# LoRA A to the head of SyncE's queue, six folds before the first tile, and the fifth tile prepared between the second and third chunk of the second expert

## The reference

```python
y   = einsum('bsi,boi->bso', x, weight[adapter_ids])      # 16 experts of 1024 x 1024
h   = einsum('bsd,nrd->nbsr', y, lora_A)                  # 8 adapters of rank 16
out = x + (y @ W.T + bias) + einsum('nbsr,nor->bso', h, lora_B * (SCALE * lora_weights))
```

## Time and profile before

| | us |
|---|---|
| median of 3 runs | 1508.62 (1508.57 to 1510.61) |
| the profiled execution, its own time | 1511.33 |
| the profiled execution, span of its instructions | 1509.7 |
| TensorE busy with matmuls | 1492.8 (99%) |
| VectorE busy | 788.1 (52%) |
| ScalarE busy | 393.2 (26%) |
| GpSimd busy | 464.4 (31%) |

### The profile page before, as it was taken

One profiled execution on the slowest core, in us unless ns is written; L12 is line 12 of the kernel. 1 busy time (PEld: TensorE's weight loads), 2 busy tenths in 40 slices (PEclk: granted clock), 3 DMA queues, 4 the chain that ended last, 5 costly groups with the idle time before them and its releaser, 6 DMA issues.

```text
span 1509.7 us, 29738 instructions
## 1 busy us (share of the span) xinstructions
PE 1492.8 (99%) x6354; PEld 1190.2 (79%) x6355; DVE 788.1 (52%) x1192; ACT 393.2 (26%) x493; POOL 464.4 (31%) x651
## 2 busy tenths in 40 slices
PE   7999999999999999999999999999999999999998
PEld 4878888888888888878788888888888888888887
DVE  7767766367777368378842333333333333333331
ACT  5244343234444244244430111111111111111110
POOL 4365433533344433534102121221211212212111
PEclk9999999999999999999999999999999999999999
DMA  9979866667787467469744555555555555555553
GB/s 279 293 202 246 221 170 164 186 185 201 202 228 197 142 185 189 156 202 239 192 148 130 142 143 140 136 148 140 133 145 141 138 143 139 144 141 134 146 139 84
DMA packets 172705, 257.90 MB, mean 171 GB/s; under 512 B 31616, under 2 KB 135552, under 8 KB 172672
## 3 DMA queue, kind: packets, MB, share of 16 engines
q1 hardware_dynamic: 128896, 138.62, 36.5%
q10 hardware_dynamic: 23360, 73.28, 16.4%
q0 software_dynamic: 20416, 45.65, 10.9%
HBM read 181.93 MB, written 75.50 MB: 171 GB/s over the span
## 4 chain that ended last, share of the span: by engine, by line
PE 94%; DVE 3%; DMA 1%; ACT 1%; issue 1%; SPq 0%; DVEq 0%; POOL 0%; ACTq 0%; POOLq 0%
PE ps L751 31%; PE ps L755 31%; PE ps L758 31%; DVE w_turn L529 1%; DMA a_sb<-in_L_ffn_lora_A_dram 1%; DMA weff<-fold_sb 1%; DVE w_lo L586 1%; DVE fold_sb L644 1%; DVE x_turn L617 0%; ACT x_hi L409 0%; ACT w_hi L401 0%; PE ps L731 0%; DVE x_lo L624 0%; ACT fold_sb L441 0%; SPq L215 0%
## 5 line engine op out<-in xcount | busy, mean ns | idle before, releaser
L751 PE MATMUL ps<-w_hi,x_hi 128*128 (+1 forms) x2096 | 533.4, 395 | 2.9 <-issue 2.9
L755 PE MATMUL ps<-w_hi,x_lo 128*128 (+1 forms) x2096 | 531.4, 394 | 0.0
L758 PE MATMUL ps<-w_lo,x_hi 128*128 (+1 forms) x2096 | 531.2, 394 | 0.0
L751 PEld LDWEIGHTS ps<-w_hi,x_hi 128*128 128x128 f32 x2096 | 392.8, 188 | 101.8 <-issue 5.4
L755 PEld LDWEIGHTS ps<-w_hi,x_lo 128*128 128x128 f32 x2096 | 392.5, 187 | 97.0
L758 PEld LDWEIGHTS ps<-w_lo,x_hi 128*128 128x128 f32 x2096 | 392.2, 187 | 96.8
L208 POOL DMA_DIRECT2D x_raw<-in_x_dram x560 | 299.1, 534 | 399.8 <-DVE x_turn L617 240.9
L617 DVE STREAM_TRANSPOSE x_turn<-x_raw 128x256 f32<-128x256 f32 x544 | 193.7, 415 | 421.8 <-DMA x_raw<-y_scr 363.8
L409 ACT ACTIVATE x_hi<-x_turn 128x512 fp32r<-128x512 f32 x272 | 166.9, 630 | 686.3 <-DVE x_turn L617 670.6
L384 POOL TENSOR_TENSOR stage<-stage,w_place 128x1024 f32<-128x1024 f32 x64 | 153.1, 2392 | 612.0 <-DMA stage<-in_x_dram 612.0
L624 DVE TENSOR_TENSOR x_lo<-x_turn,x_hi 128x512 fp32r<-128x512 f32 x272 | 180.4, 691 | 128.7 <-ACT x_hi L409 124.2
(11 more groups left out here) (71 smaller groups left out, 40.0 us busy)
## 6 DMA issues: line engine op xcount, KB each, us to landing
w_place<-in_L_cond_weight_dram SPq DMA_DIRECT2D x480, 128.0 KB, 4.4
y_scr<-stage ACTq DMA_DIRECT2D x72, 512.0 KB, 4.3
x_raw<-in_x_dram POOLq DMA_DIRECT2D x560, 64.0 KB, 3.8
x_raw<-y_scr SPq DMA_DIRECT2D x512, 64.0 KB, 2.4
stage<-in_x_dram SPq DMA_DIRECT2D x128, 256.0 KB, 3.7
out_dram<-stage ACTq DMA_DIRECT2D x126, 256.0 KB, 3.0
weff<-fold_sb POOLq DMA_DIRECT2D x8, 512.0 KB, 9.9
w_place<-weff SPq DMA_DIRECT2D x32, 128.0 KB, 3.3
```

What stands on the lines that cost most here:

```text
L751: mm(ps[b][:, cols], x_hi[b][:, t, :], hi[t], start=t == 0, stop=False)
L755: mm(ps[b][:, cols], x_lo[b][:, t, :], hi[t], start=False, stop=False)
L758: last = mm(ps[b][:, cols], x_hi[b][:, t, :], lo[t], start=False, stop=t == KT - 1)
```

## The change

Four things are reordered; no instruction is added or taken away. SyncE starts the load of LoRA A first, ahead of the loads of expert 0. TensorE runs six folds before the first tile and two in its middle, and ScalarE copies the sixth before it rounds the fifth chunk of expert 0. VectorE turns the first two chunks of expert 1, then prepares tile 4 whole, and then does the splits and the other turns without a break. ScalarE rounds tile 4 before it waits for the stores of `weff`.

```diff
             sp.dma_start(ids_i[:, :], ids.rearrange("(s a) -> s a", a=1)).then_inc(ids_loaded, 16)
-            for c in range(2):
+            sp.dma_start(a_sb[:, :], lora_a.rearrange("n r d -> (n r) d")).then_inc(a_loaded, 16)
+            for c in range(LOADS - 1):
                 load_first(sp, c, (0, 1), w0_loaded)
-            sp.dma_start(a_sb[:, :], lora_a.rearrange("n r d -> (n r) d")).then_inc(a_loaded, 16)
-            load_first(sp, 2, (0, 1), w0_loaded)
...
-            for f in range(3, 5):
+            for f in range(3, 6):
                 move_fold(f)
             round_w(0, 0, [4, 5, 6, 7])
-            for f in range(5, FOLDS):
+            for f in range(6, FOLDS):
                 move_fold(f)
...
+            round_x(4, 0)
+
             act.wait_ge(weff_ready, 16 * FOLDS)
-            round_w(1, 1, range(0, CHUNKS // 2))
-            round_x(4, 0)
-            round_w(1, 1, range(CHUNKS // 2, CHUNKS))
+            round_w(1, 1)
...
-            def prepare_w(k, par, chunks=range(CHUNKS)):
+            def prepare_w(k, par, chunks=range(CHUNKS), turned=0):
                 for c in chunks:
-                    if not (isinstance(k, int) and k == 0 and c < TURN):
+                    if c >= turned:
                         turn_w(k, c)
...
-            prepare_w(1, 1, range(0, CHUNKS // 2))
+            for c in range(TURN):
+                turn_w(1, c)
             prepare_first(4)
-            prepare_w(1, 1, range(CHUNKS // 2, CHUNKS))
+            prepare_w(1, 1, turned=TURN)
...
-            for f in range(5):
+            for f in range(6):
                 fold(f)
...
-            for f in range(5, FOLDS):
+            for f in range(6, FOLDS):
                 fold(f)
```

More of the change, by code:

```diff
@@ L635, in x_index @@
                 return n // RING - (1 if n % RING else 2)
-            prepare_w(0, 0, range(0, CHUNKS // 2))
+            prepare_w(0, 0, range(0, CHUNKS // 2), TURN)
             prepare_first(0)
```

## The result

In 21 runs each, the changed kernel took 1513.28 us (median, 1512.26 to 1513.98) and the kernel before 1511.06 (1508.4 to 1513.7). The ratio is 1.0015 with a 95% interval of 1.0008 to 1.0022: slower by 1.2 to 3.3 us, 2.2 between the medians. Against the forecast this is two results. The change was forecast at + 1.3 us. That has the right sign and lies just inside the measured interval; between the medians it is 0.9 too small. The time was forecast at 1509.9 with 1512.8 as the upper end, and is missed by 3.4. Of that 0.9 is the change, and 2.4 is the 1508.62 it was counted from: a median of three runs, where the median of 21 is 1511.06.

What follows compares the result with a forecast made beforehand. TensorE, busy 1492.8 of 1509.7 us, was taken as the bound. Late tile 4 + 2.7, opening − 1.3, register load − 0.5 and clock + 0.4 gave + 1.3 on 1508.6, so 1509.9 us, range 1506.0 to 1512.8.

Steps and rivals of the forecast that it cites:

- Tile 4 into the hole: VectorE before expert 1's splits: tile 4's loads land after the stores, first split 5.4 late, 2.73 saved later, net + 2.7 us.
- Rival A: Before expert 1's splits: the hole takes tile 4 whole if loaded by about 60.5; 6.2 us faster, 1502.4; chance 0.12.
- The opening: LoRA A first and six folds ahead: VectorE's lead 1.8 us, of which 1.3 (0 to 2.1) reaches the last weff store.
- The starting value: The unchanged kernel's time the forecast was counted from: 1508.6 us, the profiled execution being 2.7 above that median.
- The sum: Slot 6's start: + 2.7 late tile 4, − 1.3 earlier opening, − 0.5 register load, + 0.4 clock; together + 1.3 us.
- The register load and the clock: TensorE at slot 6: quicker rank load − 0.5 us (0 to − 1.16), slow running after a longer wait + 0.4 us.
- That slot 6 at full speed decides the end: TensorE hardly idles from 90.00 on, so the end moves by as much as slot 6's full-speed start.
- What slot 6 waits for: Three things end just before 90.00: slot 2's copy at 86.79, tile 6's first half about 88.1, the rank load at 89.3.
- B: At the weff stores: full DMA engines keep the earlier opening from reaching them; + 4.1 us, 1512.7; chance 0.14.
- C: Head of SyncE's queue: expert 0's first chunks 2 us late, LoRA B late, tile 0 no earlier; + 3.7, 1512.3; chance 0.05.
- D: Up to slot 6: everything cancels (opening − 2.1, register load − 1.16, tile 4 + 2.7); − 0.5 us, 1508.1; chance 0.12.

Runs made afterwards that it cites:

- experiment 1: Kernel before with only tile 4's move into the hole, opening as before: ratio 1.0026 to the kernel before.
- experiment 3: Changed kernel with tile 4's eight loads ahead of the weff stores in GpSimd's queue: 1509.0 us, ratio 0.9985 to the kernel before.
- experiment 5: Experiment 3's early loads and the new opening, but tile 4 prepared in its old place: 1512.76 us, ratio 1.001 to the kernel before.
- experiment 11: Changed kernel with tile 4's loads between the sixth and seventh weff store: 1510.19 us, ratio 0.9993 to the kernel before.
- experiment 10: Kernel before with LoRA A at the head of SyncE's queue and nothing else: ratio 0.9999 to the kernel before.
- experiment 2: Kernel before with only LoRA A first and six folds ahead, tile 4 in its old place: ratio 0.9998 to the kernel before.
- Experiment 4: The kernel before, unchanged, run and profiled once more: ratio 1.0002.
- experiment 8: Changed kernel with tile 4's eight loads on SyncE's queue, ahead of expert 1's chunks: 1511.23 us, ratio 0.9998 to the kernel before.
- experiment 6: Experiment 3 with TensorE reading the next slot's mark and rank before waiting for the present one: ratio 1.0039 to the kernel before.
- experiment 7: Kernel before with TensorE reading the next slot's mark and rank before waiting for the present one: ratio 1.0058.
- experiment 9: Experiment 3 with that early reading of mark and rank for slots 4 to 7 alone: 1506.68 us, ratio 0.9967 to the kernel before.

## Why the prediction was right and wrong

**Tile 4 into the hole: right, by experiments 1, 3, 5 and 11.** The step said that the tile is complete about 3 us after the last store, so that its move costs + 2.7. In the profile the gap is 64.5 − 61.0 = 3.5, its transposes begin at 64.56 (forecast 65.6 − 1.3 = 64.3), the first split at 67.63 (forecast 67.5). The prediction's reading that no load gets ahead of the stores was loose: the first of the eight landed at 62.0, 0.3 before the last store; it is the last of them, at 65.5, that VectorE waits for. Experiment 3 takes the cause away and the loss becomes a gain. Rival A's point from which it decides holds as well: at 55.15 there is a win, and at 61.04 (experiment 11) none that is clear. Its price, 6.2 us, was too high (experiment 3 gains 0.9 to 3.5), since the loads that get ahead delay the stores, and slot 6 waits for more than its tile.

**The opening: right in what it does, and what reaches the stores.** VectorE at tile 0: 21.74, forecast 21.8. The first turned chunk: 2.07 ahead, forecast 1.8. The last store: 62.3 to 61.0, the 1.3 that was taken; in experiment 10 ScalarE's wait ended at 61.11, but in experiment 2 only at 61.72 and the gain was gone. So the 1.3 came true here, and how much of the lead reaches the stores as a rule is not shown.

**The starting value: the larger failed step.** The sum was added to 1508.6, the median of three runs. It was not the middle of the kernel's spread: 21 runs have 1511.06, that is 2.4 of the 3.4 us by which the time was missed. The profiled execution beside the three, 1511.33, was nearer. The text set it aside as "2.7 above the median" and counted from the lower figure; counted from it, the forecast would have been 1512.6.

**The register load and the clock: the failed step within the sum.** The sum had − 0.5 for a quicker load and + 0.4 for the clock. The load was slow again, 1.561 us where the earlier trace rows have 1.462, so + 0.1 in place of − 0.5. The clock: from slot 6's start to the start of its third pass (L758) the changed kernel needs 98.08 − 91.76 = 6.32, and the kernel before 95.38 − 90.00 = 5.38, so + 0.94 in place of + 0.4:

```profile
95.38 2.03 PE L758 MATMUL ps<-w_lo,x_hi 128*128 x8
```

TensorE's idle time was forecast as one wait of 4 to 6 us before slot 6. It is 3.40 + 2.79, and with the two matmuls of slot 5 between them, already at the low clock (1.22 us instead of 0.63). With the chain at + 1.7 in place of + 1.4 (tile 6's rounding at 89.19 instead of 87.50) the profile has + 2.70 at the third pass, where the sum had + 1.3. Experiment 4 bounds what this is worth: two profiles of the kernel before differ by 1.3 at the same point, so the split is that of these two executions; the medians say + 2.2.

**That slot 6 at full speed decides the end: right.** From it to the end of the span it is 1413.8 to 1415.0 us in all eleven profiles that have no look-ahead in the loop. So the span's + 2.2, beside + 2.70 at this point, is within that scatter.

**What slot 6 waits for.** The prediction named three things that end just before it: the copy of slot 2, tile 6's rounding, and the register load of the rank. The ten profiles without a look-ahead show which it is:

| profile | copy of slot 2 ends | rank load starts | it takes | slot 6 starts |
|---|---|---|---|---|
| before | 86.79 | 87.8 | 1.46 | 90.00 |
| after | 88.44 | 89.5 | 1.56 | 91.76 |
| experiment 1 | 90.15 | 91.2 | 1.39 | 93.30 |
| experiment 2 | 87.30 | 88.4 | 1.37 | 90.44 |
| experiment 3 | 85.03 | 86.1 | 1.28 | 88.07 |
| experiment 4 | 87.68 | 88.7 | 1.84 | 91.28 |
| experiment 5 | 87.81 | 88.9 | 1.68 | 91.25 |
| experiment 8 | 86.40 | 87.5 | 1.68 | 89.84 |
| experiment 10 | 85.56 | 86.6 | 1.61 | 88.94 |
| experiment 11 | 86.14 | 87.2 | 1.16 | 89.06 |

In each the rank load starts about 1.05 us after the copy, and slot 6 starts about 0.7 after the load's end. The program has it so: TensorE waits for `moved` first, and reads the used mark and then the rank after it. Tile 6's rounding is earlier (in the changed kernel its first half is done at about 89.19 + 1.22 / 2 = 89.8). The look-ahead takes the two loads out of this path, and then tile 6's rounding is what ends TensorE's wait (experiments 6, 7 and 9).

**Rivals.** B (the opening doesn't reach the stores) has part of the truth in experiment 2. C fell: the first chunk was 0.3 late, LoRA B not at all. D's quick register load came in none of the ten profiles without the look-ahead: the rank load took 1.16 to 1.84 us. In experiment 1 the used mark took 0.312 and the rank behind it 1.386:

```profile
L197 PEldq TENSOR_LOAD <-slot_tab x2: 312/849/1386, 90.3 to 91.2; - x2
```

## What to carry to other kernels

A wait of an engine is only a hole for work whose operands are there. Before moving a block into it, read the landing time of the block's last transfer and what lies ahead of it in its queue; where the hole is itself a wait for that queue, the block arrives when the hole closes. Move the transfer first, and count what it then delays. Where an engine still waits after its operands are there, read what it does between the semaphore and its first instruction: here two register loads, which a look-ahead over four slots took off the path. And where several runs and a profiled one disagree by more than the change is worth, forecast the ratio and widen the time.

## What the runs showed of the hardware

Register loads from SBUF mostly take 0.27 to 0.31 us on SyncE, GpSimd and TensorE (their medians over the kernel before are 0.267, 0.291 and 0.307 for the largest group of each); ScalarE's and VectorE's loads of `slot_tab` have medians of 0.596 and 0.391. TensorE's load of the rank at slot 6 took 1.16 to 1.84 in each of the ten profiles without the look-ahead. Several engines' loads end together, as in the changed kernel's at 91.1 to 91.4:

```profile
L197 ACTq TENSOR_LOAD <-slot_tab x1: 1446/1446/1446, 89.8 to 89.8; - x1
L197 POOLq TENSOR_LOAD <-slot_tab x1: 1012/1012/1012, 90.3 to 90.3; - x1
L197 DVEq TENSOR_LOAD <-slot_tab x1: 923/923/923, 90.5 to 90.5; - x1
```

The DMA share there is 0.98 or more, but that alone is not the cause: from 60 to 66 in the kernel before it is 1.08, and both of TensorE's loads in it took 0.30. What makes a load slow stays open.

The clock after a wait is no fixed price: after 1.17 us of waiting in experiment 6 and 1.53 in experiment 7 the first eight matmuls took 2.13 us, after 1.64 in experiment 9 they took 3.68. From slot 6's start to its third pass it is 3.83 us in experiments 6 and 7, where the clock stayed high, and 5.29 to 6.32 in the others, so a fall costs slot 6 between 1.5 and 2.5 us.

The kernel before spreads over 5.3 us in 21 runs, the changed one over 1.7. Experiment 4 shows one source: LoRA A landed 0.7 later, and in the changed kernel nothing waits for A. It isn't the only one, since experiments 3 and 10, with LoRA A first as well, spread over 3.6 and 3.9 us.
